# Second attention of a two-layer block: the output projection in four pieces, the softmax sums and their inverses in single transfers, and PV in half key tiles throughout

## The reference, cut to what matters

```python
H = 16; Dh = 8; scale = Dh ** (-0.5)          # B, T, C = 2, 1024, 128
q = (x @ wq_w.T + wq_b).reshape(B, T, H, Dh)   # k and v likewise
scores = einsum('bthd,bshd->bhts', q, k) * scale
scores = where(key_mask, scores, -inf)
attn = softmax(scores, axis=-1)
out = einsum('bhts,bshd->bthd', attn, v).reshape(B, T, C)
return out @ wo_w.T + wo_b
```

## Time and profile before

| what | us |
|---|---|
| median of 3 runs | 1722.8 (1717.89 to 1723.13) |
| the profiled execution, own time | 1719.14 |
| its span | 1717.3 |
| first reduction of the second attention starts | 1304.8 |
| last one starts | 1634.7 |
| last exponential starts | 1679.7 |

### The profile page before, as it was taken

The page is one execution under the profiler, slowest core; times in us unless marked ns, Lnnn a source line. Parts: engine busy times, 40 slices in busy tenths (PEclk is TensorE's granted clock), DMA queues, the critical chain, the costliest instruction groups (busy, mean ns, idle before and its releaser), DMA issues.

```text
span 1717.3 us, 28177 instructions
## 1 busy us (share of the span) xinstructions
PE 1566.3 (91%) x10531; PEld 653.9 (38%) x10531; DVE 1344.3 (78%) x2075; ACT 1273.0 (74%) x2052; POOL 963.6 (56%) x661
## 2 busy tenths in 40 slices
PE   5899999999999999999999999985776899999985
PEld 2444444444444444444444444433551222222223
DVE  6687877788777877787777877767778999999946
ACT  4777888888888888888888888873242688888872
POOL 2799877878788877888787887880000000111112
PEclk9999999999999999999999999997686899999998
DMA  4011011101011111101110101000000000000001
GB/s 125 22 27 23 21 29 33 25 23 27 22 37 23 23 25 37 26 21 26 27 35 22 27 23 33 22 11 3 1 22 23 2 16 16 17 17 14 15 14 32
DMA packets 50435, 42.37 MB, mean 25 GB/s; under 512 B 26021, under 2 KB 39242, under 8 KB 50298
## 3 DMA queue, kind: packets, MB, share of 16 engines
q1 hardware_dynamic: 50298, 40.55, 10.0%
HBM read 20.27 MB, written 1.31 MB: 13 GB/s over the span
## 4 chain that ended last, share of the span: by engine, by line
PE 74%; DVE 10%; issue 9%; ACT 5%; POOL 1%; DMA 1%; SPq 1%; ACTq 0%; POOLq 0%; DVEq 0%
PE PS L1439 20%; PE PS L1451 16%; PE PS L1463 13%; PE PS L1789 4%; PE PS L1506 4%; PE PS L1487 3%; PE PS L1756 2%; DVE mxp L1345 2%; PE PS L1773 2%; PE PS L1477 2%; PE PS L1523 2%; PE PS L1729 1%; DVE region L1041 1%; ACT region L766 1%; ACT ering L935 1%
## 5 line engine op out<-in xcount | busy, mean ns | idle before, releaser
L1027 DVE TENSOR_REDUCE nmx<-PS 128x1 f32<-128x1024 f32 x512 | 622.1, 1220 | 193.3 <-PE PS L1440 193.0
L567 POOL TENSOR_TENSOR ering<-ering 128x1024 f32<-128x1024 f32 x256 | 603.4, 2357 | 21.4
L748 ACT ACTIVATE ering<-PS,nmx 128x1024 f32<-128x1024 f32 x512 | 570.3, 1114 | 42.3 <-DVE nmx L1027 41.9
L565 POOL TENSOR_SCALAR ering<-ering,rho 128x1024 f32<-128x1024 f32 x256 | 286.3, 1119 | 220.9 <-DVE rho L1036 217.9
L1439 PE MATMUL PS<-region 64*128 64x512 f16 x1536 | 404.4, 380 | 6.1 <-DMA region<-region 4.2
L1440 PE MATMUL PS<-region 64*128 64x512 f16 x1536 | 404.4, 380 | 0.0
L1451 PE MATMUL PS<-ident,ering 128*128 128x128 f32 x2048 | 334.9, 286 | 8.8 <-ACT t L759 6.4
L1345 DVE TENSOR_REDUCE mxp<-PS 128x2 f32<-128x1024 f32 x256 | 303.8, 1221 | 30.1 <-PE PS L1773 26.5
L935 ACT ACTIVATE ering<-PS 128x1024 f32<-128x1024 f32 x256 | 260.3, 1024 | 76.4 <-PE PS L1756 68.6
L1451 PEld LDWEIGHTS PS<-ident,ering 128*128 128x128 f32 x2048 | 215.5, 141 | 259.4 <-issue 222.1
L1439 PEld LDWEIGHTS PS<-region 64*128 64x128 f16 x1536 | 112.3, 94 | 248.8 <-ACT ering L748 72.2
(11 more groups left out here) (286 smaller groups left out, 1855.1 us busy)
## 6 DMA issues: line engine op xcount, KB each, us to landing
region<-region SPq DMA_DIRECT2D x64, 256.0 KB, 3.7
osb<-scr SPq DMA_DIRECT2D x32, 128.0 KB, 3.2
rcp<-scr SPq DMA_DIRECT2D x32, 128.0 KB, 3.3
rcp<-scr SPq DMA_DIRECT2D x64, 64.0 KB, 2.0
x<-in_L_attn_X SPq DMA_DIRECT2D x4, 256.0 KB, 3.1
wq_raw<-in_L_attn_Wq SPq DMA_DIRECT2D x16, 64.0 KB, 3.2
wk_s<-in_L_attn_Wk SPq DMA_DIRECT2D x16, 64.0 KB, 1.8
wo_s<-in_L_attn_Wo SPq DMA_DIRECT2D x32, 32.0 KB, 2.6
```

The source lines that it names most:

```text
L565: P.tensor_scalar(e2, e2, rho[:, s:s + 1], 1.0, ALU.mult, ALU.mult).then_inc(s_scl_ok, 1)
L567: P.tensor_tensor(e1, e1, e2, ALU.subtract).then_inc(s_sub_ok, 1)
L748: A.activation((E1, E2)[p][s % 4], PS[:, bank:bank + 2, :].rearrange("p a b -> p (a b)"), ACT.Exp, bias=nmx[:, 2 * s + p:2 * s + p + 1], s ...
L1027: V.tensor_reduce(nmx[:, 2 * s + p:2 * s + p + 1], PS[:, bank:bank + 2, :].rearrange("p a b -> p (a b)"), AX.X, ALU.max, negate=True).then ...
```

## The change

TensorE: `values1` makes half key tiles throughout, 16 pieces a half. They stand at the steps v = 4 to 8 of a half (pieces 0 to 4), two at v = 9 (5 and 6), and one each from v = 10 to 18 (7 to 15); so the doubled step is the fifth behind the first. `to_out1` makes pieces of 128 columns, four a half: for the first half at the steps 29, 30, 31 and 0 of the next block, for the second at 13 to 16. `turn_z1(0)` moves from step 2 to 4. ScalarE: the copy of the correction rows comes two steps later (5 and 21), the copy of the projection one step later (16, and 0 of the next block). VectorE: the inversion comes two steps earlier (5 and 21). SP: one transfer for the sums and one for the broadcast in place of four each, and the inverses go to DRAM before the correction rows, not behind them. The counts of the semaphores follow.

```diff
--- before.py
+++ after.py
@@ -503,34 +503,35 @@
             def sums_out1(hf):
 
                 sp.wait_ge(s_os1_ok, hf + 1)
-                for j in range(4):
-                    sp.dma_start(rc[32 * j:32 * j + 32, 0, :],
-                                 osb[32 * j + 8:32 * j + 9, :].rearrange("o (p c) -> o p c", c=16)).then_inc(s_sum_dma1, 16)
-
-            def sums_back1(hf):
-
+                sp.dma_start(rc[:, 0, :], osb[8:128:32, :].rearrange("j (p c) -> j p c", c=16)).then_inc(s_sum_dma1, 16)
+
+            def inverses_out1(hf):
                 sp.wait_ge(s_rc1_ok, hf + 1)
                 sp.dma_start(scr1.rearrange("(p c) -> p c", c=16), rc[:, 1, :]).then_inc(s_scr_dma1, 16)
+
+            def inverses_back1(hf):
+
                 sp.wait_ge(s_scr_dma1, 16 * (hf + 1))
                 if hf > 0:
                     sp.wait_ge(s_on1_ok, hf)
-                for j in range(4):
-                    sp.dma_start(rcp[32 * j:32 * j + 32, :], scr1[j * HF:j * HF + HF].rearrange(
-                        "(o q) -> o q", o=1).to_broadcast([32, HF])).then_inc(s_rcp_dma1, 16)
+                sp.dma_start(rcp[:, :], scr1.rearrange("(j o q) -> j o q", j=4, o=1).to_broadcast(
+                    [4, 32, HF])).then_inc(s_rcp_dma1, 16)
 
             for n in range(-1, last1 + 1):
                 if n >= 1:
                     sums_out1(2 * n - 1)
+                    inverses_out1(2 * n - 1)
                 if 0 <= n < last1:
                     c_rows1(n, 1)
                 if n >= 1:
-                    sums_back1(2 * n - 1)
+                    inverses_back1(2 * n - 1)
                 if 0 <= n < last1:
                     sums_out1(2 * n)
+                    inverses_out1(2 * n)
                 if n + 1 < last1:
                     c_rows1(n + 1, 0)
                 if 0 <= n < last1:
-                    sums_back1(2 * n)
+                    inverses_back1(2 * n)
             ov = out.rearrange("b (k p) e -> p (b k) e", p=128)
             for i in range(4):
                 if i < 3:
@@ -653,13 +654,13 @@
 
                 g, b = divmod(n, 2)
                 if n >= 2:
-                    pool.wait_ge(s_pv1, 30 * (n - 1))
+                    pool.wait_ge(s_pv1, 32 * (n - 1))
                 pool.wait_ge(s_v1_ev, 1)
                 P.tensor_copy(vst[:, b, :, :, 0:8], va[:, b * NT:b * NT + NT, 32 * g:32 * g + 32].rearrange(
                     "p k (j d) -> p k j d", j=4)).then_inc(s_stv_ok, 1)
 
             def weigh1(hf):
-                pool.wait_ge(s_rcp_dma1, 64 * (hf + 1))
+                pool.wait_ge(s_rcp_dma1, 16 * (hf + 1))
                 if hf > 0:
                     pool.wait_ge(s_y1_mm, hf)
                 P.tensor_tensor(on[:, :], osb[:, :], rcp[:, :], ALU.mult).then_inc(s_on1_ok, 1)
@@ -894,7 +895,7 @@
                              bias=pcol[:, 10 + 4 * qk + g:11 + 4 * qk + g]).then_inc(s_p1_x, 1)
 
             def copy_out1(hf):
-                act.wait_ge(s_pv1, 15 * (hf + 1))
+                act.wait_ge(s_pv1, 16 * (hf + 1))
                 if hf > 0:
                     act.wait_ge(s_on1_ok, hf)
                 A.activation(osb[:, :], OT, ACT.Copy).then_inc(s_os1_ok, 1)
@@ -930,21 +931,21 @@
                         c = 32 * n + t
                         act.wait_ge(s_scores1, c + 1)
                         if c >= 8:
-                            act.wait_ge(s_pv1, 15 * ((c - 8) // 16) + 2 * ((c - 8) % 16 // 2) + 1)
+                            act.wait_ge(s_pv1, 16 * ((c - 8) // 16) + 2 * ((c - 8) % 16 // 2) + 2)
                         at = score_pair(n, t)
                         A.activation(ering[:, c % 8, :, :], PS[:, at:at + 2, :], ACT.Exp,
                                      scale=SCALE1).then_inc(s_exps1, 1)
-                    if t == 3 and 0 <= n < last1:
+                    if t == 5 and 0 <= n < last1:
                         ct_copy1(2 * n + 1)
-                    if t == 19 and n + 1 < last1:
+                    if t == 21 and n + 1 < last1:
                         ct_copy1(2 * (n + 1))
                     if t == 15 and n == last1:
                         open_r(0)
                         open_r(1)
-                    if t == 15 and n >= 1:
+                    if t == 0 and n >= 1:
+                        copy_y1(2 * n - 2)
+                    if t == 16 and n >= 1:
                         copy_y1(2 * n - 1)
-                    if t == 31 and 0 <= n < last1:
-                        copy_y1(2 * n)
             open_r(2)
             open_r(3)
 
@@ -1285,7 +1286,7 @@
                              AX.X).then_inc(s_cmax1, 1)
 
             def invert1(hf):
-                dve.wait_ge(s_sum_dma1, 64 * (hf + 1))
+                dve.wait_ge(s_sum_dma1, 16 * (hf + 1))
                 if hf > 0:
                     dve.wait_ge(s_scr_dma1, 16 * hf)
                 V.reciprocal(rc[:, 1, :], rc[:, 0, :]).then_inc(s_rc1_ok, 1)
@@ -1348,14 +1349,14 @@
                         row_max1(2 * n + 1)
                     if t == 16 and n + 1 < last1:
                         row_max1(2 * (n + 1))
-                    if t == 7 and n >= 1:
+                    if t == 5 and n >= 1:
                         invert1(2 * n - 1)
                     if t == 7 and n == last1 - 1:
                         norm4(0)
                         mix(0)
                         square(0)
                         norm4(1)
-                    if t == 23 and 0 <= n < last1:
+                    if t == 21 and 0 <= n < last1:
                         invert1(2 * n)
                     if t == 23 and n == last1 - 1:
                         mix(1)
@@ -1777,17 +1778,17 @@
             def values1(n, qh, k, half):
 
 
-                if k == 0:
+                if k == 0 and half == 0:
                     if qh == 0:
                         pe.wait_ge(s_stv_ok, n + 1)
                     if 2 * n + qh > 0:
                         pe.wait_ge(s_os1_ok, 2 * n + qh)
                 pe.wait_ge(s_exps1, 32 * n + 16 * qh + 2 * k + 2)
-                at = slice(256 * half, 256 * half + (HF if k == 0 else 256))
+                at = slice(256 * half, 256 * half + 256)
                 for i in range(4):
                     c = 16 * qh + 2 * k + i % 2
                     mm = MM(OT[32 * i:32 * i + 32, at], vst[:, n % 2, k, i, :], ering[:, c % 8, i // 2, at],
-                            start=(k == 0), stop=(k == 7 and half == 1))
+                            start=(k == 0 and half == 0), stop=(k == 7 and half == 1))
                 mm.then_inc(s_pv1, 1)
 
             def spread1(hf):
@@ -1798,9 +1799,9 @@
 
             def to_out1(hf, part):
                 pe.wait_ge(s_on1_ok, hf + 1)
-                at = slice(256 * part, 256 * part + 256)
+                at = slice(128 * part, 128 * part + 128)
                 mm = MM(MISC[:, at], wo1[:, hf // 4, :], on[:, at], start=True, stop=True)
-                if part == 1:
+                if part == 3:
                     mm.then_inc(s_y1_mm, 1)
 
             def four(bank, done, op):
@@ -1846,24 +1847,30 @@
                         maxima1(n + 1, t)
                     if t < 3 and n >= 1:
                         values1(n - 1, 1, (t + 13) // 2, (t + 13) % 2)
-                    if t % 16 == 4 and own:
-                        values1(n, t // 16, 0, 0)
-                    if (5 <= t < 19 or t > 20) and own:
-                        values1(n, t // 20, (t - 16 * (t // 20) - 3) // 2, (t - 3) % 2)
+                    if (4 <= t < 19 or t >= 20) and own:
+                        qh = t // 20
+                        v = t - 16 * qh
+                        for q in (v - 4,) if v < 9 else (5, 6) if v == 9 else (v - 3,):
+                            values1(n, qh, q // 2, q % 2)
                     if t == 3 and own:
                         if n >= 1:
                             pe.wait_ge(s_yc1_ok, 2 * n - 1)
                         spread1(2 * n + 1)
-                    if t in (14, 15) and n >= 1:
-                        if own:
-                            pe.wait_ge(s_ct_ev1, 2 * n + 2)
-                        to_out1(2 * n - 1, t - 14)
+                    if t == 0 and n >= 1:
+                        to_out1(2 * n - 2, 3)
+                    if t == 13 and own and n >= 1:
+                        pe.wait_ge(s_ct_ev1, 2 * n + 2)
+                    if 13 <= t < 17 and own and n >= 1:
+                        to_out1(2 * n - 1, t - 13)
+                    if t == 14 and n == last1:
+                        for part in range(4):
+                            to_out1(2 * n - 1, part)
                     if t == 19 and nxt:
                         if n >= 1:
                             pe.wait_ge(s_yc1_ok, 2 * n)
                         spread1(2 * (n + 1))
                     if n == last1 - 1:
-                        if t == 2:
+                        if t == 4:
                             turn_z1(0)
                         if t == 10:
                             turn_x4(0)
```

(8 more changed lines are left out.)

## The result

The changed kernel takes 1742.8 us (median of 4 runs, 1741.3 to 1745.5) against 1721.9 for the kernel before in the same series: a ratio of 1.0129, 95% interval 1.0114 to 1.0145. It is slower by 1.3%, and the time lies outside the range of the prediction. The profiled execution took 1743.7, its span 1741.9.

A forecast was written before the change was run, and what follows sets the result against it. A two-step loop of scores, exponential, maxima and PV, 2.40 us with 0.1 slack a step, sets the pace. Halves go from 21.10 to 21.36: +3.4, n = 7 -3.0, tail -1.5, total -1.1, so 1721.7 us; range 1714 to 1732.

The forecast's parts named there:

- Projection, +0.01 a half against the two parts: Four steps with 128-column pieces at 0.41 us each on TensorE take 6.06 us, against 6.05 with two parts.
- PV, the term for the doubled step: Steps 9 to 12 of a half become 5.21 us from 4.78; the doubled step costs its whole 0.43 there.
- Sums in one transfer: Row sums land 2.0 to 2.5 us after issue; in n = 7 they are there some 2.5 us earlier.
- I take 3.5 to 4.3, hidden: The single broadcast of the inverses lands 3.5 to 4.3 us after issue, costing nothing in the halves.
- rival (a): Single broadcast, carried by four engines, lands late at 4.5 to 5.2 us: +2 to +10.9, middle +6, 1728; chance 0.32.
- deadline of 4.36: Time the broadcast may take from issue before POOL's product delays the first piece at v = 13.
- n = 7, -3.0: Last block, where nothing is reduced: earlier sums remove waits, less what is given back; -3.0 us (0 to -4.5).
- -4.3, -0.5, +0.7, +0.9, +0.4, +0.2: n = 7: ScalarE stop and clock loss; z transposes at v = 2; v = 4; doubled steps; first piece; second z transposes.
- Tail, -1.5: Chain from last copy over sums and reciprocal to norm: three issues of 0.62 go, 0.3 longer landing comes; -1.5 us.
- Rival (b): Projection pieces cost only 0.31 to 0.35 us and the ends gain all they can: -6.3, 1716.5 us; chance 0.17.

The follow-up runs named there:

- third run: Changed kernel with the broadcast back in four transfers and `parts1` ahead of `add_out1` in POOL's program: 1720.9 us, ratio to before 1.0006.
- ninth run: Kernel before with sums in one transfer, later copy of y, `parts1` before `add_out1`, `turn_z1(0)` at step 4, plus the projection in four pieces: 1718.6 us (0.9998).
- sixth run: Kernel before with only PV in half key tiles and the doubled step at v = 9: 1718.2 us, ratio to before 0.9991.
- fourth run: Kernel before with only the sums in one transfer: 1714.3 us, ratio to before 0.9953.
- seventh run: Changed kernel with `parts1` ahead of `add_out1` and the broadcast in two transfers of two heads each: 1815.7 us, ratio to before 1.0555.
- first run: Changed kernel with the broadcast of the inverses back in four transfers: 1725.5 us, ratio to before 1.0026.
- second run: Changed kernel with `parts1` ahead of `add_out1` in POOL's program, in both halves: 1737.2 us, ratio to before 1.0084.

## Why the prediction was wrong

By its steps:

- **Projection, +0.01 a half against the two parts**: the piece was right (0.41 measured). Without the two waits the whole half came to 21.31 (third run) for 21.36. But the half before isn't 21.17 everywhere, as the prediction and the section on the profile before have it: it lasts 21.30 and 21.25 in n = 1 and 2, 21.21 and 21.17 from n = 3 on, and n = 0 is a shorter block, about 41. What the step left out is that the first piece is due a step earlier, so that the margin of the broadcast shrinks for any form of it (third and ninth runs).
- **PV, the term for the doubled step**: 0.15 a half too dear; measured even (sixth run).
- **Sums in one transfer**: right. 1.9 us to land in n = 7, for 2.0 to 2.5, and worth -3.8 and -1.2 where nothing else is changed (fourth run), for the forecast's -3 and -1.5.
- **"I take 3.5 to 4.3, hidden"**: this step failed. The single broadcast lands in 5.0 (4.65 to 5.37 in 16 halves), by four engines, which is rival (a), with a chance of 0.32. Its deadline of 4.36 was right (4.26 in the third run), its landing of 4.5 to 5.2 too. The Trainium skill's rule of the slowest dimension ("DMA: Bandwidth & Descriptors", "Why a DMA increments its semaphore by 16 and not by 1") is borne out by the shares of 0.25 and 0.13 and by the small packets. It also says that the engines taken are the lowest-numbered ones; that the two transfers of the seventh run share two engines agrees with it, though no view here shows the engines' numbers. The 3.5 to 4.3 came from transfers of 32 rows each, which say nothing of one with another outermost count.
- **The price of rival (a)**: also too small. I priced lateness in the loop only, at 6 in the middle of 2 to 10.9; taking it away gave 8.2 in the loop and 6.3 in n = 7. There the product is on the path as well: the stop of 1.95 at v = 13, then half the clock, then 4.38 at t = 29.
- **POOL's order, nowhere in the prediction**: I moved the copy of y by a step and costed it on ScalarE and TensorE, but didn't follow it into POOL's program, where `add_out1` waits for it and `parts1` stands behind. 0.48 a half from n = 3 on, 3.8 us in eight halves (first run), of which the late broadcast hides about half in the changed kernel (1.8 in the second run).
- **n = 7, -3.0**: the terms as the prediction lists them (-4.3, -0.5, +0.7, +0.9, +0.4, +0.2) add up to -2.6, not to -3.0. Measured: -3.8 for the sums alone; +7.9 with all of the change. Besides the product, 0.2 was put for the second z transposes, which waited 1.17 for the later copy of y. The norm of the second tokens stands behind them (1684.02 to 1689.2 on VectorE), and the reciprocal of the last but one half behind the norm (as it does in the kernel before), at 1689.28, though its sums were issued at 1684.28. With both waits taken away n = 7 still is 45.8, 4.7 above the fourth run. The pieces with their earlier deadline (+3.6 in the ninth run) and the half key tiles (+1.4 in the sixth) are about that, for 0.4 and 0.9 in the prediction.
- **Tail, -1.5**: +0.6. The sums are 1.7 sooner as forecast (issue to reciprocal 1.8 for 3.5), but the broadcast takes 1.8 more, and the inverses' write 2.0 more (see the last section). That makes +2.1 up to the product. How it shrinks to +0.6 behind it is open: the tail of single executions varies, from 35.4 (ninth run) to 38.5 (first run).
- **Rival (b)** at 1716.5 left out the tail's -1.5, and would have been 1715.0; it didn't come true.

## What to carry to other kernels

When an instruction is moved, follow its result into every engine's program and look at what stands behind the instruction that waits for it: here a copy that came one step later held up, on a third engine, work that had nothing to do with it. Before transfers are joined, write down the outermost count of the joined pattern: four rows of sums (8 KB) gained by it, a broadcast of 256 KB with four heads outermost lost more than three issues cost. A deadline moved up by one step doesn't show in the typical half, but in those where the transfer takes a microsecond more (21.45 to 21.93 for 21.32 in the third run).

## What the runs showed of the hardware

The write of the inverses (8 KB) took 1.4 us to land in nearly all halves of the kernels built on the one before. In the changed kernel and its four direct variants (first, second, third and seventh run) it took 2.6 to 3.5 in the last two halves, with the same instructions around it on SP. The DMA view of the changed kernel from 1689.5 to 1692.7, that is from that write's issue at 1689.56 to the broadcast's at 1692.67:

```profile
DMA packets 145, 0.02 MB, mean 8 GB/s; under 512 B 144, under 2 KB 144, under 8 KB 144
## 3 DMA queue, kind: packets, MB, share of 16 engines
q1 hardware_dynamic: 144, 0.01, 3.2%
q8 instruction: 1, 0.02, 2.7%
...
scr<-rc SPq DMA_DIRECT2D x1, 8.0 KB, 3.1
```

The same stretch of the fourth run's kernel (1664.1 to 1665.8):

```profile
DMA packets 144, 0.01 MB, mean 5 GB/s; under 512 B 144, under 2 KB 144, under 8 KB 144
## 3 DMA queue, kind: packets, MB, share of 16 engines
q1 hardware_dynamic: 144, 0.01, 5.4%
...
scr<-rc SPq DMA_DIRECT2D x1, 8.0 KB, 1.4
```

One packet of instructions (16 KB) is in the first and none in the second. 2.7% of 16 engines over 3.2 us is 1.4 us of one engine, about what the landing is longer by. The order of the packets shows where the write stood. In the DMA view of the changed kernel no packet starts from 1690.7 to 1691.6, and the view from 1691.6 to 1692.6 has the rest of the write:

```profile
DMA packets 9, 0.00 MB, mean 1 GB/s; under 512 B 9, under 2 KB 9, under 8 KB 9
```

Nine is a sixteenth of 144, the share of one engine. It starts when the packet of instructions, which runs from 1690.22 to 1691.62, has ended. The traces of all eleven kernels have 14 such writes that took more than 2.5 us to land, and it is the same in each of them: one instruction packet of 0.9 to 1.5 us, and 9 packets of the write behind its end. None of the other 162 writes took more than 2.3. So one engine's share stands behind the instructions, and the landing waits for it. No run moved the instruction packet, but no case speaks against this. It is worth 1.7 to 2.0 us at each of the two places in the changed kernel, and it explains the single long writes elsewhere (2.85 in the ninth run).

The late landings of the broadcast in four transfers go with it too. In the second attention of the kernels that have it, it took 4.0 us or more in 19 halves, and in each of the 19 a packet of instructions of 0.9 to 1.4 us lies between issue and landing. In the 74 without one it never took more than 3.6. The other 19 have a packet that is short or comes near the end, and took 3.3 to 4.0.
